# Zeros for the gathered rows: one long transfer, or eight that keep step with the attention

## The reference

```python
x = x + attn_a(layernorm(x))   # 8 batches of 256 rows of 128; 8 heads; softmax over the queries
x = x + ffn(layernorm(x))      # each of the 2048 rows goes to one of 8 experts (the largest gate)
x = x + attn_b(layernorm(x))   # 16 heads of 8, rotary, masked by pages of 32
x = x + ffn(layernorm(x))      # the same experts once more

def ffn(x):                    # what the change is about
    probs = softmax(x @ w_gate + b_gate)
    e, p = argmax(probs), max(probs)
    return (relu(x @ W1[e] + b1[e]) @ W2[e] + b2[e]) * p
```

## Time and profile before

| | |
|---|---|
| Runs | 467.4, 468.68, 468.87 us |
| Profiled execution: its own time | 468.14 us |
| Its span, first to last instruction | 466.2 us |
| Mean granted TensorE clock | 0.91 of full speed |
| PE busy | 405.4 us (87% of the span) |
| DVE, ACT, POOL busy | 301.8, 232.5, 214.6 us |
| Bytes moved | 28.72 MB, of them 20.90 MB on SP's queue |

### The profile page before, as it was taken

How to read it: one execution, slowest core, us unless ns; L and a number is a source line. 1 busy time by engine, 2 the same in 40 slices (tenths; PEclk the granted TensorE clock), 3 DMA queues, 4 the chain that set the end, 5 groups by cost and what they waited for, 6 DMA issues and landing times.

```text
span 466.2 us, 15366 instructions
## 1 busy us (share of the span) xinstructions
PE 405.4 (87%) x5230; PEld 317.2 (68%) x5231; DVE 301.8 (65%) x1081; ACT 232.5 (50%) x573; POOL 214.6 (46%) x335
## 2 busy tenths in 40 slices
PE   8999799998857799999679998999988889899980
PEld 8877578886645788986446665665655567699870
DVE  5777588888745445427858777778776555555443
ACT  1587556666411455524327765766555420355540
POOL 4443335666343144447754754654622444144440
PEclk9999999999755999999859998999898776899996
DMA  8999940000000121212000000000000000121216
GB/s 246 279 208 302 291 121 16 13 11 11 13 13 23 51 60 57 68 38 83 1 1 1 2 1 1 3 2 3 1 1 14 24 24 23 42 59 57 68 39 191
DMA packets 44614, 28.72 MB, mean 62 GB/s; under 512 B 7344, under 2 KB 40752, under 8 KB 44560
## 3 DMA queue, kind: packets, MB, share of 16 engines
q1 hardware_dynamic: 38368, 20.90, 16.3%
q0 software_dynamic: 2496, 5.13, 3.2%
q10 hardware_dynamic: 3696, 1.97, 1.4%
HBM read 12.83 MB, written 15.16 MB: 60 GB/s over the span
## 4 chain that ended last, share of the span: by engine, by line
PE 59%; DVE 17%; issue 8%; DMA 6%; ACT 4%; DVEq 2%; POOL 2%; SPq 1%; POOLq 0%; ACTq 0%
PE S L1471 7%; PE banks L1481 6%; PE S L1379 6%; PE banks L1338 5%; PE banks L1355 3%; PE banks L1513 3%; DVE nm L767 3%; PE banks L1596 3%; PE banks L1365 2%; PE S L1311 2%; PE S L1567 2%; DMA slots<-yo,token 2%; PE S L1566 2%; DMA xg<-rows 2%; PE banks L1290 2%
## 5 line engine op out<-in xcount | busy, mean ns | idle before, releaser
L937 ACT ACTIVATE E<-S,nmax 128x256 f32<-128x256 f32 x128 | 59.0, 477 | 40.9 <-DVE nmax L551 40.9
L1194 POOL DMA_INDIRECT slots<-yo,token x46 | 44.1, 958 | 72.5 <-DVE yo L707 71.8
L1032 ACT ACTIVATE E<-S 128x1536 f32<-128x1536 f32 x32 | 46.4, 1451 | 25.7 <-PE S L1572 25.7
L1153 POOL TENSOR_TENSOR vs<-Va,rden 128x512 f32<-128x512 f32 x32 | 33.3, 1040 | 49.2 <-DVE rden L586 47.8
L1471 PE MATMUL S<-xgT,W1s 128*128 128x128 f32 x368 | 51.4, 282 | 1.5 <-DVE xgT L693 1.3
L994 ACT ACTIVATE hT<-S,b 128x128 f32<-128x128 f32 x92 | 28.7, 363 | 40.8 <-PE S L1471 40.8
L1481 PE MATMUL banks<-W,hT 128*128 x368 | 48.8, 276 | 0.2
L767 DVE TENSOR_REDUCE nm<-banks 128x2 f32<-128x512 f32 x64 | 40.9, 680 | 12.2 <-PE banks L1539 12.2
L1471 PEld LDWEIGHTS S<-xgT,W1s 128*128 128x128 f32 x368 | 44.5, 191 | 4.7 <-issue 2.2
L1481 PEld LDWEIGHTS banks<-W,hT 128*128 128x128 f32 x368 | 44.8, 192 | 0.5 <-issue 0.5
L551 DVE TENSOR_REDUCE nmax<-S 128x4 f32<-128x1024 f32 x32 | 39.0, 1218 | 9.4 <-PE S L1379 9.0
(11 more groups left out here) (185 smaller groups left out, 947.9 us busy)
## 6 DMA issues: line engine op xcount, KB each, us to landing
rows<-zeros SPq DMA_DIRECT2D x1, 8768.0 KB, 34.4
xg<-rows SPq DMA_DIRECT2D x46, 64.5 KB
W<-in_L_ffn_W SPq DMA_DIRECT2D x1, 2048.0 KB, 10.3
x<-in_L_attn_a_x SPq DMA_DIRECT2D x4, 256.0 KB, 5.3
yg<-slots SPq DMA_DIRECT2D x8, 128.0 KB, 3.4
yg<-slots ACTq DMA_DIRECT2D x8, 128.0 KB, 3.7
slots<-yo,token POOLq DMA_INDIRECT x46
yg<-in_select SPq DMA_DIRECT2D x1, 512.0 KB, 7.7
```

Of the source, the lines that this page charges most:

```text
L937: last = act.activation(E[:, hp, h, c, :], S[hp % 2][:, h, c * T:(c + 1) * T], ACT.Exp, bias=nmax[:, hp, k:k + 1], accum_out=den[:, hp, k: ...
L1032: act.activation(Eb[:, q % 2, :, :], S4[:, 0:3, :], ACT.Exp, scale=SCALE_B).then_inc(bs["exp"], 1)
L1194: pool.indirect_dma_start(out=y_dram, out_offset=bass.IndirectOffsetOnAxis(token[:, turn_at, :], 0), in_=yo[:, turn_at % 2, :], in_offset=None
```

## The change

The table is no longer filled by one transfer. A new SBUF tile `wide` of 258 words per partition (two rows of the table) is zeroed by POOL, and eight transfers of 128 x 8 pieces of 1032 bytes each write the k-th 256 places of all eight experts. The k-th is issued when `a_scores` has reached 3k + 1 and the one before has landed. W1 and W2 are loaded expert by expert, one at `a_scores` 3k + 2 and one at 3k + 3. Behind these 24 transfers come the 896 rows at the table's end, then b1, b2, and `wo` as before. `scatter(0, c)` waits on POOL for the first c + 1 transfers of zeros; the wait for all of them moves from POOL (ahead of the loop) to SP, ahead of the first load of a tile. The expert weights count on a semaphore of their own, `weights`, for which PE, DVE and ACT wait at the start of the first expert layer; `w_loaded` keeps only the gate's two transfers.

```diff
@@ SP
-            sp.dma_start(W1[:, :, :], W1_in.rearrange("e d m -> d e m")).then_inc(w_loaded, 16)
-            sp.dma_start(W2[:, :, :, :], W2_in.rearrange("e (c p) d -> p e c d", p=P)).then_inc(w_loaded, 16)
+            sp.wait_ge(wide_zero, 1)
+            places = flat[0:NE * REGION * W].rearrange("(e k p c) -> k p e c", e=NE, k=B, p=P)
+            for g in range(1, 3 * B + 1):
+                e, kind = divmod(g - 1, 3)
+                sp.wait_ge(a_scores, g)
+                if kind == 0:
+                    if e > 0: sp.wait_ge(slots_zero, 16 * e)
+                    sp.dma_start(places[e], wide[:, :].unsqueeze(1).to_broadcast([P, NE, 2 * W])
+                                 ).then_inc(slots_zero, 16)
+                elif kind == 1:
+                    sp.dma_start(W1[:, e, :], W1_in[e]).then_inc(weights, 16)
+                else:
+                    sp.dma_start(W2[:, e, :, :], W2_in[e].rearrange("(c p) d -> p c d", p=P)).then_inc(weights, 16)
+            sp.wait_ge(slots_zero, 16 * B)
+            sp.dma_start(flat[NE * REGION * W:ROWS * W].rearrange("(p k c) -> p k c", p=P, c=W),
+                         wide[:, 0:W].unsqueeze(1).to_broadcast([P, SLOTS - NT, W])).then_inc(slots_zero, 16)
             sp.dma_start(b1[...], ...)                      # now counts on weights
             sp.dma_start(b2[...], ...)                      # now counts on weights
-            sp.wait_ge(pool_const, 1)
-            sp.dma_start(flat.rearrange("(p k d) -> p k d", p=P, d=D),
-                         zeros[:, :].unsqueeze(1).to_broadcast([P, CHUNKS, D])).then_inc(slots_zero, 16)
...
@@ SP, ffn_loads(n), ahead of the first tile
+                if n == 0:
+                    sp.wait_ge(slots_zero, 16 * (B + 1))
@@ DVE and PE, ahead of the loop of batches 3 to 6
-            dve.wait_ge(w_loaded, 96)
+            dve.wait_ge(w_loaded, 32)
@@ PE, DVE and ACT, ahead of ffn_tiles(0)
+            pe.wait_ge(weights, 16 * (2 * NE + 2))
@@ POOL
+            pool.memset(wide[:, :], 0.0).then_inc(wide_zero, 1)
...
+                if n == 0:                                  # in scatter(n, c, p)
+                    pool.wait_ge(slots_zero, c * 16 + 16)
...
-            pool.wait_ge(slots_zero, 16)                    # ahead of the loop
```

More of the change, by code:

```diff
@@ L122, in build @@
         zeros = sb("zeros", [P, D])
+        wide = sb("wide", [P, 2 * W])
         lg = sb("lg", [P, 2, NE])
@@ L243, in build @@
         slots_zero = sem("slots_zero")
+        wide_zero = sem("wide_zero")
+        weights = sem("weights")
         named = sem("named")
@@ L382, in _ @@
             sp.dma_start(bg[:, :], bg_in.unsqueeze(0).to_broadcast([P, NE])).then_inc(w_loaded, 16)
-            sp.dma_start(W1[:, :, :], W1_in.rearrange("e d m -> d e m")).then_inc(w_loaded, 16)
-            sp.dma_start(W2[:, :, :, :], W2_in.rearrange("e (c p) d -> p e c d", p=P)).then_inc(w_loaded, 16)
-            sp.dma_start(b1[:, :, :].rearrange("p e c -> p (e c)"), b1_in.rearrange("e (c p) -> p (e c)", p=P),
-                         allow_slow_non_contiguous=True).then_inc(w_loaded, 16)
-            sp.dma_start(b2[:, :, :], b2_in.unsqueeze(0).to_broadcast([P, NE, D])).then_inc(w_loaded, 16)
-            sp.wait_ge(pool_const, 1)
-            sp.dma_start(flat.rearrange("(p k d) -> p k d", p=P, d=D),
-                         zeros[:, :].unsqueeze(1).to_broadcast([P, CHUNKS, D])).then_inc(slots_zero, 16)
+            sp.wait_ge(wide_zero, 1)
[14 more added lines that the diff above has]
+                         wide[:, 0:W].unsqueeze(1).to_broadcast([P, SLOTS - NT, W])).then_inc(slots_zero, 16)
+            sp.dma_start(b1[:, :, :].rearrange("p e c -> p (e c)"), b1_in.rearrange("e (c p) -> p (e c)", p=P),
+                         allow_slow_non_contiguous=True).then_inc(weights, 16)
+            sp.dma_start(b2[:, :, :], b2_in.unsqueeze(0).to_broadcast([P, NE, D])).then_inc(weights, 16)
             for g in range(HB):
@@ L725, in _ @@
             ffn_weights(0)
+            dve.wait_ge(weights, 16 * (2 * NE + 2))
             ffn_tiles(0)
@@ L1004, in _ @@
             ffn_exp(0)
+            act.wait_ge(weights, 16 * (2 * NE + 2))
             ffn_tiles(0)
@@ L1416, in _ @@
                     a_step(b, hp, b % 2, b > 0, True)
-            pe.wait_ge(w_loaded, 96)
+            pe.wait_ge(w_loaded, 32)
             with pe.Fori(0, 2) as h:
```

## The result

The changed kernel takes 464.17 us, the median of 12 runs (457.51 to 467.43), against 469.57 for the kernel before, timed beside it (465.66 to 473.07, 12 runs). The ratio is 0.985, with an interval of 0.980 to 0.990: a gain that is clear of no change, and under 2%. The ratio and its interval are of the fast runs alone, those within 1.5% of the fastest of their kernel: seven of the changed kernel's 12, and the profiled one (465.02 us) is not among them. In a second session it was 0.984 (0.979 to 0.989; 464.58 against 471.94 us).

A forecast was written before the change was run, and what follows sets the result against it. PE was taken to bound the first attention, held up by instructions late behind the zeros. 468.14 - 4.34 (stalls gone) + 0.4 (chunks meeting code requests) = 464.2 us; own range 462.2 to 466, 8 in 10 within 462.0 to 468.2.

The forecast's parts named there:

- What held PE up: First attention, batches 2 and 3: PE ran dry because its next instructions stood behind the zeros; four stalls, together 4.34 us.
- the four of the prediction: Four "issue" stalls of PE at 41 to 63 us in the kernel before: 0.78, 0.98, 2.30 and 0.28 us.
- That the stalls go: First attention: all 4.34 us come back, less 0.4 for four meetings of code requests with chunks at 0.1 each.
- The length of a chunk: Zeros in the first attention: each 1032 KB chunk takes 4.05 us at the long transfer's rate, 5.2 at W1's.
- The weights, the memset and the waits at nothing: Moving weights from 12 to 30 us, POOL's 258-column memset, and POOL's and SP's new waits were each counted at nothing.
- the 6.6 allowed: POOL's scatters in the first attention: behind a whole chunk one would land after 6.6 us instead of 2.5, at no cost.
- The clock at 0, bounded by 1.6: TensorE's fall to the lower clock in batch 7's beginning: bounded at 1.6 us either way, taken as 0.
- The sum: Whole kernel: the profiled execution's 468.14 us - 4.34 + 0.4 = 464.2 us.
- No change: Rival: stalls belong to the zeros' traffic, whatever its length; 4.1 of 4.34 us remain, time 467.9; chance 0.12.
- Half: Rival: chunks meet PE's need for code once or twice, about 2.2 us of stalls remain, time 466.3; chance 0.13.
- Slower: Rival: chunks reach batches 3 to 5; four cost 2.30 us each, 9.2 against 4.34 gained, time 473.0; chance 0.09.
- the rule: DMA engines go round queues packet by packet; code requests never wait for a whole backlog, so shortening it gains nothing.

The follow-up runs named there:

- the long transfer (98.98): Changed kernel with the zeros as one 8768 KB transfer in 512-byte pieces again, started at step 5, weights still paced: stage 98.98 us, total 466.55.
- the second profiles: Kernel before and changed kernel each profiled once more, unedited: stage (first score of batch 0 to that of batch 7) 98.20 and 92.07 us.
- weights first: Changed kernel with W1 and W2 as two 2 MB transfers at 12 us again, zeros still paced in eight: stage 92.97 us, total 469.61.
- fours: Changed kernel with the eight chunks of zeros in two groups of four, at steps 1 and 13: stage 106.14 us, total 474.49.
- pairs: Changed kernel with the eight chunks of zeros in four groups of two, at steps 1, 7, 13 and 19: stage 102.85 us, total 469.48.
- rows: Changed kernel, still paced, with each chunk written in 516-byte pieces of one row, as two transfers: stage 118.82 us, total 487.00.
- the extra zeros at step 21: Changed kernel plus 4096 KB of zeros to a spare table, started at step 21 (about 80 us): stage 92.26 us, total 459.49.

## Why the prediction was right, and where it was not

**What held PE up: right.** The stalls are PE's code behind the zeros. They return with the long transfer (98.98), they repeat (98.20), and the same traffic costs 4.3 us or nothing, by whether PE runs through code for the first time. The fetch has rows of its own: 40 of 43 stalls end 1.2 to 1.7 us behind a packet of instructions, the four of the prediction among them.

**That the stalls go: right, and a little more.** I had 4.34 less 0.4, 3.9 us; the stage gave 4.75, and 6.1 between the second profiles, some of it the lower clock in the second profile of the kernel before. 0.2 of "issue" and some 0.8 in batch 4 were left in the first profile, the latter all but missing in the second (batch 4: 13.79 us).

**The length of a chunk: wrong, and with it the margin.** I took 4.05 us at the long transfer's rate, with 5.2 as the other end. It landed after 7.7. The rate was of aligned pieces, and the chunks' aren't. "The stall needs a backlog that has grown for longer than a chunk lasts" came out for one chunk, but for another reason: by the estimate above a packet's wait stops growing at some 4.6 us under the long transfer, and what decides is whether it exceeds what PE has in hand. I had the 11.5 us without a stall from aligned pieces, and two chunks in a row already cost 10 us. The change works with less room than the sum had. The Trainium skill, "DMA: Bandwidth & Descriptors", section on how a descriptor splits into AXI transactions, says that a descriptor that doesn't start at a multiple of 256 bytes wastes part of its first transaction. By that, as an estimate, a piece of 1032 bytes takes five transactions instead of the four of 1024 aligned bytes. That section tells of reads, and these are writes; the landing times, 7.7 against 4.6, are a larger step.

**The weights, the memset and the waits at nothing: right.** 92.97 with the weights early; `wide`'s memset took 0.32 us and the first score came at 14.53 us against 14.60; the first load, behind the wait for the zeros, follows the last scatter by the same 3.4 us as before (its transfer of 2.39 against 2.36 us included); POOL's scatters landed later (3.8 against 2.5 us), within the 6.6 allowed.

**The clock at 0, bounded by 1.6: the size was off.** It gave 1.9 us behind batch 7, and the second expert layer lost 3.1, of which the clock is at least a part. So the first load came at 143.82 us where I had 146.5. Both profiles of before have the early fall in batch 7 and neither of the changed kernel has it, but two variants of the changed one do (weights first, and fours). In these four the way from batch 7 to the first load takes 38.4 to 38.5 us, in the other ten profiles 36.5 to 37.3. Whether the change moves it regularly stays open.

**The sum: right, partly by luck.** 464.2 was forecast and 464.17 measured, but the kernel before measured 469.57, not the 468.14 on which the sum stood. The forecast's gain was 3.9 us; the medians differ by 5.4, and the ratio of 0.985 would be 7 us. In the profile the gain, 3.2 us of span, is so near the forecast because two terms that the sum had at nothing, 1.9 gained and 3.1 lost, go against each other.

**The rivals.** "No change" is refuted: the eight chunks take 7.7 us each, longer together than the 34.4 us of the long transfer, and their stalls are nearly gone. "Half" had 2.2 us left; 0.2 to 0.3 us of "issue" were, and the 0.8 in one of two profiles. "Slower" was no fancy: as pairs, fours or rows the same pacing costs 10 to 26 us of the stage against the changed kernel, and the whole takes 487.00 us with rows, more than any run of the kernel before (465.55 to 475.78); fours, 474.49, lies at the top of these.

What stays open: why writing zeros holds PE's code up for longer than loading the weights at the same DMA share (some 4.6 against 2.9 us, by the estimate above), and why the wait stops growing. The Trainium skill, "DMA: Bandwidth & Descriptors", section on queues, rings and completion order, weighed in the prediction, has a turn for each queue, packet by packet. A wait that stops growing fits such turns better than a request that waits out the whole backlog; no run here shows how long a turn is. What the prediction made of the rule, that a shorter backlog would gain nothing, didn't come out: the stage gained 4.75 us, with the changed kernel's waits at 2.9 us or less by the estimate.

## What to carry to other kernels

Before pacing a long transfer, look at whether the engine that bounds the stage runs code for the first time there: "issue" on it, under a full DMA row, was its own instructions late here, and the packets of the instruction queue can be held against each stall. Put long background writes under a second turn of a loop whose code the engine still holds, where 4096 KB cost nothing, or cut them so short that the engine bridges them. And keep the pieces of such a write on multiples of their size: that was worth 9 us of the stage in one long backlog, and 0.6 to 1.25 us paced.

## What the runs showed that I had not expected

- Writes in pieces at odd addresses land much later: 1032 KB in 7.7 us (1032-byte pieces), 1024 KB in 4.6 (1024-byte, aligned). In one long backlog they cost the stage 14.6 us instead of 5.5.
- A code stall of 3.48 us was followed by 5 us at the lower TensorE clock (0.50), so that fours lost 7.8 us in a batch whose stalls add to 4.9.
- Under the extra zeros at step 21 PE ran two batches without a gap at a DMA share of 0.98 and 0.97.
